# Cross attention on one core: two query products ahead of each chunk's first round of maxima

## What is computed

```
query = x @ Wq;  keyt = enc @ Wk;  valt = enc @ Wv
hs = mha(query, keyt, valt)
ca_q1 = einsum('btc,th->bch', ca, Wq_ca)[:, indices, :]      # 4 tokens, 384 rows spread over 2048
ca_hs1 = mha(ca_q1, x, x)
ca_hs2 = mha(ca_hs1 @ Wq, ca @ Wk_ca, ca @ Wv_ca)
out = (hs + ca_hs2) @ Wout + b_out + x
```

## Time and profile before

| | |
|---|---|
| median of 3 runs | 1533.13 us (1532.41 to 1534.29) |
| the profiled execution | 1533.26 us, its span 1531.5 us |
| TensorE busy | 1497.2 us, 98% |
| VectorE busy | 789.5 us, 52% |
| ScalarE busy | 621.2 us, 41% |
| mean granted clock of TensorE | 0.999 |

### The profile page before, as it was taken

How to read it: one execution, slowest core, us unless ns; L and a number is a source line. 1 busy time by engine, 2 the same in 40 slices (tenths; PEclk the granted TensorE clock), 3 DMA queues, 4 the chain that set the end, 5 groups by cost and what they waited for, 6 DMA issues and landing times.

```text
span 1531.5 us, 24564 instructions
## 1 busy us (share of the span) xinstructions
PE 1497.2 (98%) x10310; PEld 1244.0 (81%) x10310; DVE 789.5 (52%) x1596; ACT 621.2 (41%) x1311; POOL 2.8 (0%) x12
## 2 busy tenths in 40 slices
PE   7999999999999999999999999999999999999998
PEld 5764799999975489999987549999998745999998
DVE  6785435344478353443448826435345873453533
ACT  2438623333244852333332584324233377333322
POOL 0000000000000000000000000000000000000000
PEclk9999999999999999999999999999999999999999
DMA  6640011120252001140045100213004410021101
GB/s 237 225 157 1 7 57 66 54 112 27 104 186 101 1 19 53 57 155 21 27 144 171 67 1 20 95 38 143 9 35 167 170 37 2 19 96 58 61 18 44
DMA packets 46680, 117.28 MB, mean 77 GB/s; under 512 B 3661, under 2 KB 5317, under 8 KB 45019
## 3 DMA queue, kind: packets, MB, share of 16 engines
q1 hardware_dynamic: 37036, 93.91, 17.5%
q10 hardware_dynamic: 9535, 21.80, 3.7%
HBM read 77.33 MB, written 39.17 MB: 76 GB/s over the span
## 4 chain that ended last, share of the span: by engine, by line
PE 91%; DVE 4%; ACT 2%; issue 1%; DMA 1%; SPq 0%; ACTq 0%
PE ps_w L519 47%; PE ps_s L519 19%; PE ps_t L519 16%; PE ps_t L529 6%; PE ps_w L529 4%; DVE unit_max L1337 2%; ACT work L1141 1%; PE ps_s L529 1%; ACT ot L1055 0%; DMA xc<-in_L_xattn_Wv_ca_dram 0%; DMA xc<-in_x_dram 0%; DVE ca_mat L1353 0%; DVE ot L1449 0%; ACT ot L1124 0%; DVE xt_l L1363 0%
## 5 line engine op out<-in xcount | busy, mean ns | idle before, releaser
L519 PE MATMUL ps_w<-wo_h,ot 128*128 128x320 f32 x1280 | 310.4, 314 | 0.6 <-DVE ot L1449 0.6
L1337 DVE TENSOR_REDUCE unit_max<-ps_s 128x1 f32<-128x512 f32 x384 | 240.6, 683 | 52.5 <-PE ps_s L519 51.0
L1111 ACT ACTIVATE work<-ps_s,neg_max 128x150 f32<-128x150 f32 x512 | 152.1, 402 | 223.4 <-DVE neg_max L1395 223.4
L519 PEld LDWEIGHTS ps_w<-wo_h,ot 128*128 128x128 f32 x1280 | 220.2, 188 | 0.9 <-DVE ot L1449 0.9
L519 PE MATMUL ps_w<-wo_l,ot 128*128 128x320 f32 x640 | 197.4, 308 | 0.0
L519 PEld LDWEIGHTS ps_w<-v_all,work 120*128 120x128 f32 x1280 | 170.3, 190 | 3.0 <-issue 2.5
L519 PE MATMUL ps_w<-v_all,work 120*128 120x162 f32 (+1 forms) x1280 | 171.3, 288 | 0.0
L1391 DVE TENSOR_REDUCE neg_max<-ps_s 128x6 f32<-128x900 f32 x64 | 70.0, 1094 | 165.2 <-PE ps_s L519 165.2
L519 PE MATMUL ps_s<-keys_h,qt_h 128*128 128x300 f32 (+1 forms) x448 | 140.0, 313 | 0.0
L519 PE MATMUL ps_s<-keys_h,qt_l 128*128 128x300 f32 (+1 forms) x448 | 131.5, 293 | 0.0
L519 PE MATMUL ps_s<-keys_l,qt_h 128*128 128x300 f32 (+1 forms) x448 | 131.1, 293 | 0.0
(11 more groups left out here) (171 smaller groups left out, 2350.0 us busy)
## 6 DMA issues: line engine op xcount, KB each, us to landing
xc<-in_x_dram SPq DMA_DIRECT2D x32, 1280.0 KB, 6.6
out_dram<-work ACTq DMA_DIRECT2D x64, 320.0 KB, 2.2
xt_all<-work SPq DMA_DIRECT2D x60, 256.0 KB, 2.2
xt_l<-xt_all SPq DMA_DIRECT2D x12, 1280.0 KB, 5.6
y_all<-in_L_xattn_Wk_dram SPq DMA_DIRECT2D x4, 960.0 KB
y_all<-in_L_xattn_Wv_dram SPq DMA_DIRECT2D x4, 960.0 KB
pick<-pick_all SPq DMA_DIRECT2D x16, 194.0 KB
xc<-in_L_xattn_Wq_dram SPq DMA_DIRECT2D x1, 1600.0 KB, 10.7
```

The lines of the kernel that those rows point to most:

```text
L519: return nc.tensor.matmul(out, lhs, rhs, start=start, stop=stop, skip_group_check=True)
L1111: return nc.scalar.activation(probs[:, h * KEYS:(h + 1) * KEYS], ps_s[:, bank, c * KEYS:(c + 1) * KEYS], exp, bias=neg_max[:, s % 2, h:h + ...
L1337: v.tensor_reduce(unit_max[:, a, n, q:q + 1], bank, AX_X, ALU.max).then_inc(max_free, 1)
```

## The change

Three numbers of the table of fills move, and a new table, `Q0_FIRST`, puts 2 of a step's queries ahead of the round that follows piece 8, 13 and 18, the first round of chunks 0, 1 and 2. Summed over all places there are 75 queries as before.

```diff
-Q0_FILL = [0] * 6 + [3, 0, 4, 3, 2, 1, 2, 4, 4, 2, 2, 3, 4, 4, 1]
+Q0_FILL = [0] * 6 + [3, 0, 5, 2, 2, 1, 2, 5, 4, 2, 2, 2, 6, 4, 1]
+Q0_FIRST = {8: 2, 13: 2, 18: 2}
 Q0_ENDS = (6, 12, 17)
-Q0_SPLIT, Q0_TURNED, Q0_TRIPLE = 9, 3, 5
+Q0_SPLIT, Q0_TURNED, Q0_TRIPLE = 7, 3, 5
...
-                    if m in Q0_ENDS:
-                        queries0(done, Q0_FILL[m])
+                    ahead = Q0_FILL[m] if m in Q0_ENDS else Q0_FIRST.get(m, 0)
+                    queries0(done, ahead)
                     triple(AFTER_TURNED)
...
                     triple(AFTER_PRODUCTS)
-                    if m not in Q0_ENDS:
-                        queries0(done, Q0_FILL[m])
+                    queries0(done + ahead, Q0_FILL[m] - ahead)
                     done += Q0_FILL[m]
                     triple(AFTER_QUERIES)
```

## The result

The changed kernel took 1545.7 us (median; 1545.34 to 1548.25) where the kernel before took 1533.55 (1532.41 to 1534.29): a ratio of 1.0083, 95% interval 1.0066 to 1.0101. It is slower, as forecast, but by 12 us instead of 4.6, above the range. The profiled execution was 1548.25, its span 1546.5, 15.0 more than the span before.

What follows compares the result with a forecast made beforehand. TensorE, busy 1497.2 of 1531.5 us, was taken as the bound, with VectorE pacing parts. Per batch 0.06 + 0.46 + 0.52 + 0.11 = 1.15 us, four batches 4.6, on median 1533.13 gave 1537.7; range 1534.8 to 1539.6.

Steps and rivals of the forecast that it cites:

- said: 1.15: Whole stage, per batch: chunk 0, chunk 1, chunk 2 and the stage's end together 1.15 us slower; four batches 4.6 us.
- said +0.06: Chunk 0, per batch: 0.46 us saved at the first round comes back as waits for maxima, leaving it 0.06 slower.
- said +0.46: Chunk 1, per batch: q1.0 waits for L1358, 0.84 us, less 0.46 for two fewer queries, plus 0.08: 0.46 slower.
- said +0.52 and 0.1: Chunk 2: L1358 wait 0.98 us less 0.46, 0.52 slower; stage end: q3.0 waits for ScalarE's copy, 0.1 more; per batch.
- The maxima took chunk 0's saving back: Chunk 0: U5 and U11 wait for VectorE's earlier reductions, so of 0.46 us saved, 0.46 returns as waits.
- the bank's release by L1358: Chunks 1 and 2: the new group's first query waits for VectorE's L1358 to free its ps_w bank; 0.7 to 0.9 us each.
- the second row: List of waits: weight loads of the ps_s matmuls waited 59.5 us for VectorE's reductions (L1337), so VectorE sets the pace in places.
- One fall of the clock more, 4.6 + 1.6: Rival 3: the new waits bring one more fall of TensorE's clock, costing 1.6 us; 1539.3 us, chance 0.14.
- no row told its cause: Batch 2's stage: one stretch at granted clock 0.73 took 6.30 us against 4.70 in batch 1, a 1.6 us fall, cause unknown.
- borne out little: Skill's clock rule: longer waits could bring more falls; 12 waits up to 0.4 us and 4 up to 0.6 came with one fall.

Runs made afterwards that it cites:

- e9_after_with_unread: The whole changed kernel plus one 128x512 matmul nobody reads in step 8 and one in step 9; 1539.85 us, ratio 1.0044 to the kernel before.
- e1_chunk0_only: The kernel before with two queries ahead of the first round in chunk 0 alone, chunks 1 and 2 as before; 1552.14 us, ratio 1.0107.
- n1_group_end_behind_turn: Against the kernel before, another dealing: last three queries of groups 0 and 1 behind the turn of g, one of group 0 ahead of U0; 1544.49 us.
- after: The changed kernel itself, with two queries ahead of the first rounds of chunks 0, 1 and 2, against the kernel before; 1545.7 us, ratio 1.0083.
- e7_unread_for_missing: Chunk 0 alone changed against the kernel before, plus one matmul nobody reads in step 8 and one in step 9; ratio 1.0001, ten runs 1530.67 to 1534.43.

## Why the prediction was wrong

**Right, by its own steps.** The order costs 1.17 to 1.25 us per batch at full clock (said: 1.15). Between the copies of g, batch 0 shows it chunk by chunk: from chunk 0's to chunk 1's 14.72 us for 14.73 (said +0.06), to chunk 2's 15.76 for 15.26 (+0.50; said +0.46), to chunk 3's 12.58 for 11.90 (+0.68; said +0.52 and 0.1), to the end 10.57 in both. The 0.1 at the end came from another wait than walked: q3.0 waited for nothing, but the turn of g, which had stood 3.31 us behind products 19, stood 2.95 behind them instead of 2.85, held by VectorE's split, though I had said that behind piece 19 nothing of VectorE is waited for. That it has the same size is luck in part; both waits hang on the same copies by ScalarE. The maxima took chunk 0's saving back, seen in the wait at 439.11; the bank's release by L1358 set q1.0 and q2.0, up to 0.9 us of idle time at their weight loads; the rest of the kernel stayed as it was. The direction came from these. (The 59.5 us that the prediction calls the second row are its third.)

**Wrong, and the step that failed.** "One fall of the clock more, 4.6 + 1.6" was the term that was mis-sized, and with it the chance of the range. I took the price of a fall from the only one in the trace, 1.6 us, and let at most one come or go. Measured: a fall can go on for 23.9 us and cost 9.8 (62.27 against 52.48) where the one of the kernel before lasted 3.4, and the changed kernel's profiled run has a long one and a short one in batch 2 and a short one in batch 3 (13.98 and 14.01 us between the copies of g for chunks 2 and 3, for 12.58), worth 12.2 us against 1.6 before. Behind it is a step of the reasoning: in chunk 0 I counted work against waits, found 0.46 us in each, and set the result to 0.06. In time that was right. But a wait for a reduction in place of a query means that TensorE does less in that stretch, and there so small a difference decided whether the clock held. The kernel before gave the sign, with its fall in the like stretch behind chunk 2's first round (from 842.4, 8.7 us behind the copy of g at 833.70; the earlier trace rows have it in a window at 0.73); I wrote that no row told its cause and moved on. The right reading was that the stage has such stretches, in chunk 0 and behind chunk 2's first round, and that a fall there can cost 1.6 us or several times that. With chunk 0's falls kept away (`e9_after_with_unread`, 1539.85 us) the time is near what one fall more was to give, 1539.3.

The Trainium skill (TensorE: Matmul & The Clock Gate, What's actually happening) has the rule that TensorE's activity is what keeps the clock up. I weighed it against the waits of up to 0.6 us in the list and found it borne out little. The experiments bear it out in chunk 0, where I didn't look: eight matmuls in the place of waits for maxima kept the long falls away in ten runs of ten. Elsewhere they don't show it: three in the place of each wait on L1358 left falls in seven places of the profiled run, and through the long fall of the changed kernel TensorE was busy, by the profile, 23.90 of 23.90 us and stayed at the lower level.

**What stays open.** A fall costs 9.8 us in one batch and 1.6 in another of the same kernel (62.27 and 54.11 in `e1_chunk0_only`) because it lasts 23.9 us in the one and 3.4 in the other. Why isn't settled; no run tells what ends it. What starts it is known by place only: apart from `n1_group_end_behind_turn`, all 25 falls of the profiled runs begin 8.1 to 9.8 us behind the copy of g for chunk 0 or chunk 2, never behind that for chunk 1 or 3. What in TensorE's work counts isn't settled either. From U0 to the fall in batch 1 of `e1_chunk0_only`, and over the like stretch of the kernel before, where the clock held, the profile's busy times are

```profile
430.38:438.20 7.82, 7.72 (x47) 5.41 (x47) 6.72 (x11) 1.48 (x3) 0.00 (x0) 1.00 0.47 136
```

```profile
431.31:439.13 7.82, 7.72 (x49) 5.56 (x49) 6.27 (x11) 1.54 (x3) 0.00 (x0) 1.00 0.46 135
```

7.72 of 7.82 us both where it fell and where it held; only the number of matmuls differs, 47 and 49. The busy share doesn't show which of the two is going to fall; the modelled ends of matmuls can hide waits. And the split between step 8 and step 9 was only narrowed down: two in step 9 came with a fall in chunk 0 in the profiled run of each of the six kernels that had it without the unread matmuls, five in both steps with three in step 9 went with three long executions of ten, of which no trace shows where they fell. What in the order of chunk 2 adds falls there isn't known.

## What to carry to other kernels

Work that is moved into one wait leaves another stretch; look whether a third engine paces that stretch, for then it only turns into waits there. Here filler among such waits also kept the matmul engine's clock up. So before thinning a stretch look for a fall of the granted clock anywhere in similar stretches of the trace, and let the range hold several of them, long ones. A first instruction of a group carries the release of its buffer with it: moved ahead, it is the buffer's reader that decides when all the work behind it starts.

## What the runs showed of the hardware

TensorE's clock fell to its lower level in stretches where the profile calls it busy throughout, and it could stay there for 23.9 us although the profile shows work all the time (`after`, 814.4 to 838.3: 23.90 us busy of 23.90, at 0.50). The falls of the profiled runs lasted 3.4, 6.8, 13.7, 17.1 or 23.9 us. The same instructions in the same order were at full clock in one batch and at 0.81 over the stage in the next of the same run (`e1_chunk0_only`, batches 0 and 1). Eight matmuls of 0.4 us each, whose results nobody reads, came with a median of 1533 us for 1552 (`e7_unread_for_missing` and `e1_chunk0_only`).
